# The low part of K on VectorE instead of GpSimd, in an attention and mixture-of-experts block of 32 examples

## What is computed

```python
h = layernorm(x) * (1 + ca) + sa
q, k, v = rotate(rot_w[0], h), rotate(rot_w[1], h), rotate(rot_w[2], h)
attn = softmax((2 + 2 * (q @ k.T)) / scale + bias)
ave = attn @ v
x = x + ga * ave / norm(ave)
h = layernorm(x) * (1 + cb) + sb
x = x + gb * (routed_experts(h, top_k(softmax(h @ gate_w.T))) + shared(gelu(h @ Wsg.T) * (h @ Wsu.T)))
```

## Time and profile before

| what | us |
|---|---|
| median of 3 executions | 2378.26 |
| lowest and highest | 2375.60 and 2378.57 |
| the profiled execution | 2380.66 |
| its span, first to last instruction | 2378.6 |
| TensorE busy in it | 2233.8 |
| VectorE busy | 1660.2 |
| GpSimd busy | 1470.9 |
| ScalarE busy | 1158.4 |

### The profile page before, as it was taken

One profiled execution on the slowest core, in us unless ns is written; L12 is line 12 of the kernel. 1 busy time (PEld: TensorE's weight loads), 2 busy tenths in 40 slices (PEclk: granted clock), 3 DMA queues, 4 the chain that ended last, 5 costly groups with the idle time before them and its releaser, 6 DMA issues.

```text
span 2378.6 us, 40049 instructions
## 1 busy us (share of the span) xinstructions
PE 2233.8 (94%) x13432; PEld 1954.5 (82%) x13432; DVE 1660.2 (70%) x3117; ACT 1158.4 (49%) x2138; POOL 1470.9 (62%) x1156
## 2 busy tenths in 40 slices
PE   5799999999999999999989999999999999999997
PEld 4688888888788878888878888888888888888886
DVE  6788888999999999999765554545555554554543
ACT  4566666667666666566443333333333333333332
POOL 3666666666766766766545666666666666666664
PEclk8899999999999999999999999999999999999999
DMA  3212112122122112112154443444443444443433
GB/s 100 72 57 74 71 64 76 65 70 75 58 74 80 57 68 84 58 69 75 55 124 83 87 86 59 87 90 83 89 87 58 85 89 83 88 88 58 86 62 45
DMA packets 83202, 179.59 MB, mean 76 GB/s; under 512 B 12320, under 2 KB 47296, under 8 KB 83072
## 3 DMA queue, kind: packets, MB, share of 16 engines
q0 software_dynamic: 49152, 67.14, 17.7%
q1 hardware_dynamic: 33600, 109.98, 13.6%
q10 hardware_dynamic: 320, 0.56, 0.1%
HBM read 110.29 MB, written 67.34 MB: 75 GB/s over the span
## 4 chain that ended last, share of the span: by engine, by line
PE 57%; POOL 20%; issue 12%; DVE 7%; ACT 3%; DMA 1%; POOLq 0%; DVEq 0%; ACTq 0%; SPq 0%
PE ps L385 17%; PE ps L386 17%; PE ps L387 17%; DVE stage L1071 3%; POOL x_rows L1397 3%; POOL v_f L1356 3%; POOL weights L1374 3%; POOL v_f L1362 3%; POOL hidden L1341 2%; PE ps L538 2%; PE ps L473 1%; POOL rstd L1350 1%; POOL out_factor L1427 1%; PE ps L426 1%; ACT weights L716 1%
## 5 line engine op out<-in xcount | busy, mean ns | idle before, releaser
L385 PE MATMUL ps<-x_t,weights 128*128 128x512 f32 x1536 | 611.3, 398 | 11.1 <-DVE hidden_f L1305 4.2
L1441 POOL DMA_INDIRECT out<-x_rows,step_token x256 | 418.4, 1634 | 324.0 <-DVE x_rows L1285 265.2
L386 PE MATMUL ps<-x_t,weights 128*128 128x512 f32 x1536 | 600.9, 391 | 0.0
L387 PE MATMUL ps<-x_t,weights 128*128 128x512 f32 x1536 | 599.6, 390 | 0.0
L385 PE MATMUL ps<-weights,hidden 128*128 128x256 f32 x2048 | 585.2, 286 | 4.9 <-DVE hidden L1312 2.3
L386 PE MATMUL ps<-weights,hidden 128*128 128x256 f32 x2048 | 580.6, 284 | 0.0
L387 PE MATMUL ps<-weights,hidden 128*128 128x256 f32 x2048 | 580.5, 283 | 0.0
L1305 DVE TENSOR_TENSOR hidden_f<-gelu,ps 128x512 f32<-128x512 f32 x256 | 175.6, 686 | 385.8 <-ACT gelu L868 385.8
L868 ACT ACTIVATE gelu<-ps 128x512 f32<-128x512 f32 x256 | 152.4, 595 | 551.6 <-PE ps L387 551.6
L385 PEld LDWEIGHTS ps<-weights,hidden 128*128 128x128 f32 x2048 | 393.3, 192 | 15.5 <-issue 2.9
L386 PEld LDWEIGHTS ps<-weights,hidden 128*128 128x128 f32 x2048 | 393.5, 192 | 7.3
(11 more groups left out here) (160 smaller groups left out, 3838.2 us busy)
## 6 DMA issues: line engine op xcount, KB each, us to landing
pairs<-mod_rows SPq DMA_DIRECT2D x36, 512.0 KB, 3.7
x_rows<-in_x SPq DMA_DIRECT2D x32, 512.0 KB, 3.5
h_rows<-stage SPq DMA_DIRECT2D x32, 512.0 KB, 2.6
out<-y_rows SPq DMA_DIRECT2D x32, 512.0 KB, 2.8
value_mods<-value_rows SPq DMA_DIRECT2D x32, 384.0 KB, 3.4
stage<-in_wg SPq DMA_DIRECT2D x16, 512.0 KB, 3.6
stage<-in_wd SPq DMA_DIRECT2D x16, 512.0 KB, 6.2
stage<-in_wu SPq DMA_DIRECT2D x16, 512.0 KB, 4.9
```

What stands on the lines that cost most here:

```text
L385: pe.matmul(o, lhs(HI), rhs(HI), start=start, stop=False)
L386: pe.matmul(o, lhs(HI), rhs(LO), start=False, stop=False)
L387: return pe.matmul(o, lhs(LO), rhs(HI), start=False, stop=stop)
L1441: pool.indirect_dma_start(out=out_rows, out_offset=bass.IndirectOffsetOnAxis(ap=ICUR[g][:, t:t + 1], axis=0), in_=X1[:, g % 2, t * D:(t + ...
```

## The change

`k_split_lo` moves from GpSimd's program to VectorE's. On GpSimd it stood behind the sum into `y_rows` (L1415) and ahead of the factor (L1427); on VectorE it stands behind `hidden(i - 1, 0)` and ahead of the early rounds and `out_norm`. The semaphores and the waits on both sides stay. 31 subtractions of 128x1024 move, those for examples 1 to 31.

```diff
+            def k_split_lo(n):
+                dve.wait_ge(k_hi, n + 1)
+                split_lo(K_FLAT[:, LO, :], K_F[:, :, :].rearrange("p k s -> p (k s)"),
+                         K_FLAT[:, HI, :]).then_inc(k_lo, 1)
...
                 if valid(i - 1):
                     hidden(i - 1, 0)
+                if valid(i + 1) and not at(i, -1):
+                    k_split_lo(i + 1)
                 if at(i, B):
                     first_weights_lo((0, 2), 5)
                 for g, r, before in early:
...
-            def k_split_lo(n):
-                pool.wait_ge(k_hi, n + 1)
-                pool.tensor_tensor(K_FLAT[:, LO, :], K_F[:, :, :].rearrange("p k s -> p (k s)"),
-                                   K_FLAT[:, HI, :].bitcast(F32), ALU.subtract).then_inc(k_lo, 1)
...
-                if valid(i + 1) and not at(i, -1):
-                    k_split_lo(i + 1)
                 if valid(i):
```

More of the change, by code:

```diff
@@ L1231, in iteration @@
                     h1_split_lo(0)
-                    dve.wait_ge(k_hi, 1)
-                    split_lo(K_FLAT[:, LO, :], K_F[:, :, :].rearrange("p k s -> p (k s)"),
-                             K_FLAT[:, HI, :]).then_inc(k_lo, 1)
+                    k_split_lo(0)
                 if at(i, 0):
```

## The result

| what | before | changed |
|---|---|---|
| median, us | 2378.14 | 2383.81 |
| lowest and highest | 2375.60 and 2379.66 | 2381.28 and 2388.09 |
| executions | 8 | 8 |
| the profiled execution | 2380.66 | 2381.28 |
| its span | 2378.6 | 2379.2 |

The ratio of the changed kernel to the one before is 1.0031, with a 95% interval of 1.0021 to 1.0041. It is **slower**, by 5.7 us between the medians (which alone make 1.0024). By this sample the growth is just beyond the 0.2% of the likeliest case, so the second case came true and not the first, which had the higher chance.

A forecast was written before the change was run, and what follows sets the result against it. Regular iterations were taken as bound by ScalarE's squares, iterations 0, 18 and 26 to 30 by VectorE. Terms -1.0 + 4.2 + 1.0 + 0 = +4.2 us on a median of 2378.26 gave 2382.5 us, range 2376 to 2387.

The forecast's parts named there:

- the likeliest case: The terms as summed: 2382.5 us, with 2377.1 to 2383.0 within 0.2% of the time before; chance 54%.
- the second case: The shift passes whole in iterations 18 and 26, 1.06 us each, small start gain: +6.2 us, 2384.5 us, slower; 39%.
- GpSimd's share of the chain is not a gain: Regular iterations: removing 31 subtractions of 2.407 us from GpSimd is worth nothing, since its next operation waits for norm_sq.
- The norm chain waits for the squares: Regular iterations: norm_sq's operation still waits for ScalarE's squares, leaving VectorE 1.0 us of slack; term 0.
- L1041's block: VectorE's 128x4 operation stood blocked behind GpSimd's subtraction, 2.33 us against 0.15.
- Iterations 27 to 30: VectorE is late there and the 1.06 us shift reaches TensorE's wait: 4.2 us slower in all, bounds 1.6 to 4.6.
- The start: Iteration 0, bound by VectorE: unblocked v_cross lets norm_sq's operation start earlier, 1.0 us faster, bounds 0 and twice that.
- Iterations 18 and 26: Early round, no late one: later hidden and score_rows delay TensorE by 0.5 us each, 1.0 us slower; bounds 0.3 and 1.06 each.
- The sum: -1.0 + 4.2 + 1.0 + 0 = +4.2 us, by the ends of the terms -1.2 to +6.7.
- The second rival: Same as the second case: +6.2 us, decided if iterations 18 and 26 cost more than 0.8 us each; 39%.
- The third rival: GpSimd's row is what matters, so 74 us go, to about 2304 us; 2%.
- The fourth, the lock: Regular iterations: L1041 no longer blocked gains 1.0 us in each of 24, 25 us in all, 2353 us; 1%.

The follow-up runs named there:

- not_early: Changed kernel, but the subtraction stays on GpSimd in iterations 18 and 26 to 30 and moves in the other 25; 2377.42 us against 2378.36, ratio 0.9994.
- twice: Changed kernel plus one more equal subtraction on VectorE, into an unread buffer, in the 24 regular iterations; 2385.53 us against 2378.79 before the change, ratio 1.0028.
- thrice: Changed kernel plus two more equal subtractions on VectorE, into unread buffers, in the 24 regular iterations; 2418.20 us against 2378.79 before the change, ratio 1.0160.
- only_early: Changed kernel, but the subtraction is on VectorE only in iterations 18 and 26 to 30; 2385.00 us against 2378.36 before the change, ratio 1.0028.
- again: The changed kernel measured and profiled once more, no edit; 2383.07 us against 2378.36 before the change, ratio 1.0022.
- after_rstd: Changed kernel with the second layer norm's factor moved ahead of v_shift on GpSimd; 2378.90 us against 2377.75 before the change, ratio 1.0004.
- fill: Changed kernel, but the subtraction is on VectorE only in iteration 0; 2377.55 us against 2378.36 before the change, ratio 0.9995.
- behind_norm: Changed kernel with the subtraction behind out_norm instead of ahead of it in every iteration; 2378.63 us against 2378.79 before the change, ratio 1.0000.
- control: Kernel before the change with only GpSimd's iterations unrolled in the code, same order of work; 2376.90 us against 2378.79, ratio 0.9995.
- mix: Changed kernel with the subtraction ahead of out_norm in iteration 0 and behind it elsewhere; 2378.62 us against 2377.75 before the change, ratio 0.9998.
- mix_rstd: Kernel mix with the second layer norm's factor also moved ahead of v_shift on GpSimd; 2373.63 us against 2377.75 before the change, ratio 0.9984.
- before_rstd: Kernel before the change with only the second layer norm's factor moved ahead of v_shift on GpSimd; 2374.35 us against 2377.75, ratio 0.9983.

## Why the prediction was right, and where it wasn't

**GpSimd's share of the chain is not a gain: right.** 31 subtractions left GpSimd and no iteration from 2 to 17 or 19 to 25 moved by more than 0.02 us. `not_early` shows it alone.

**The norm chain waits for the squares: right.** L1049's bracket names them in 25 iterations. The slack of 1.0 us was measured as a wait of 1.04 us; `twice` used it up and `thrice` overran it.

**L1041's block was GpSimd's subtraction: right.** It takes 0.15 us now, 0.16 at most, in all 32. As the prediction said, this alone is worth nothing where the squares are late, and 0.9 us in iteration 0.

**Iterations 27 to 30: right in place, cause and size.** 1.14, 1.12 (28 taken as 29, without the clock), 1.12 and 0.94 us, 4.3 in all where the sum had 4.2. `only_early` gives the same within 0.02 us.

**The start: mis-sized.** The term was -1.0. The first transposes came 0.91 us earlier, but 0.50 were given back in iteration 1, so the term was -0.4. The prediction took the whole gain to come off because TensorE waits 8.1 us there, and expected that wait to shrink to 7.1; it grew to 8.53. What follows it runs at the low level of the clock, and the end of that stretch did not come earlier with its start: the granted clock is 0.50 up to 78.9 us in both traces. Since `only_early` has nearly as much without the move, the 0.50 us is not shown to belong to the change.

**Iterations 18 and 26: mis-sized.** The term was 0.5 us each, 1.0 in all, and measured 1.60 and 0.21. The argument for 0.5 was that TensorE stood ahead of the scores of iteration 18 for 0.34 us of "issue" with no semaphore, so that a later `score_rows` would be absorbed in part. It was not: with `score_rows` 1.2 us later TensorE waits 0.82 us for it by name. In the trace of before the wait was over or nearly so when TensorE came, and a wait that ends in time leaves no bracket. Slack has to be read from the two ends: 708.96 + 1.08 = 710.04 us for `score_rows` and 710.79 for the scores, 0.75 us apart. But in the changed kernel, where TensorE waits for `score_rows` by name, its scores too start 0.66 us behind the end of it (710.15 + 1.07 = 711.22, and 711.88). So of the 0.75 us only 0.09 was slack, and `not_early`, with VectorE 0.35 us late and no bank wait, loses 0.54. Of the 1.60 us the hole in VectorE's row is 0.3 to 0.4: `only_early` and `twice` have none and grow by 1.32 and 1.24. It stands in none of the prediction's steps; the other 1.2 to 1.3 us are still more than twice the term. In iteration 26 the scores come 1.04 us later as well, but the idle time ahead of L1071 takes in 0.8 of it. The prediction priced the two by one wait, that at the scores, and looked at none behind it. This is read from the traces; no run takes that idle time away.

**The clock: missing.** 1.46 us in iteration 28. No term, no rival had it. Every trace with the subtraction on VectorE ahead of the early rounds has such a stretch in iterations 28 to 30 (the changed kernel, `again`, `only_early` and `after_rstd` in 28, `twice` in 30, `thrice` in 29 and 30; `after_rstd` has another in 31), and of the others only `fill` has one between iterations 2 and 31.

**The sum.** -0.4 + 0.1 + 1.6 + 0.2 + 4.3 + 1.5 = 7.3 us against +4.2. The three misses all went the same way: 0.6 at the start, 0.8 in 18 and 26, 1.5 by the clock. The second rival had +6.2 and named iterations 18 and 26 and a small gain at the start as what would decide. Together 18 and 26 cost 1.81 us where it had 2.1, and the start gave little, but not in its way: the shift passed whole in 18 only, and the clock, which it didn't have, did more than either. That the measured median still lies 1.3 us from the forecast is in part luck: stage A of the traces grew by 3.1 us more than the sum, and the medians by 1.5 more.

The third rival, by which the chain was right, is refuted by `not_early`: 25 subtractions left GpSimd and the time stayed. The fourth, the lock, holds in iteration 0 alone, as it was put.

**What stays open.** The hole of 0.48 us in iteration 18: `changed` and `again` have it behind MAX8, `not_early` and `behind_norm` have 0.35 us elsewhere in the same round, `control`, `fill`, `only_early` and `twice` have none. `after_rstd` has it as the changed kernel has, and `mix` and `mix_rstd` have it as `behind_norm` has. So it repeats wherever VectorE's program is the same, and no semaphore accounts for it; that it is how the program lies in memory is a guess which no run tests. And what makes the clock fall: the stretches at the start of an iteration stand behind waits of 1.95 to 2.3 us, and `fill` has one behind 1.77 us, while `behind_norm` and `mix` have waits of 1.78 us, the changed kernel one of 2.00 and `thrice` two of 2.14, without one. A longer wait makes it likelier in these traces, but the six stretches in the middle of iterations of `thrice` follow two waits of 0.76 and some 0.7 us close together. What decides is not settled.

## What to carry to other kernels

An operation is free or costs its full length by its place in the row, not by the engine's load: look for the wait that it can stand in, and then go through the iterations that differ from the rule, since six odd ones here cost more than 25 regular ones could give. Moving work off an engine gains nothing where its consumer waits for a third party, and the bracket that will be left is found by comparing the ends of all that the consumer waits for. A wait that isn't in a trace is not slack: work it out from when the producer ended and from how long the engine takes from a release to its start (0.66 us here, of 0.75 that looked free). Then look at the next wait behind it, which may take the shift in, as in iteration 26, or not, as in 18.

## What the hardware showed that was not expected

**A tiny operation pays the whole price.** On VectorE, 128x4 took 2.33 us in place of 0.15, and in `before_rstd` 128x2 took 2.37 in place of 0.28, each until a GpSimd operation of 2.4 to 2.7 us had ended.

**Two VectorE operations in a row shut GpSimd out once.** The factor was held by the first of two 1.22 us operations and ended while the second ran at its usual length. The Trainium skill (page "SBUF — State Buffer", section "Who interferes with whom") says that a VectorE instruction with two SBUF inputs contends with a GpSimd one that reads SBUF, by an exclusive lock on the shared ports; that the first to issue has them for the whole instruction while the other blocks it says of VectorE's two-port modes. With the first subtraction the trace agrees with such a lock: 1.93 us for the factor against 1.01 alone. Were the lock held for the whole of the factor too, the second VectorE operation, which starts at 596.26, should have stood still until the factor's end at 597.22; it ended at 597.48 after its usual 1.22 us. So here a lock for the whole instruction is not what is measured.

**TensorE's clock falls in the middle of a dense kernel.** Behind a wait of 1.96 us the granted clock of the next 4.4 us was 0.61, and transposes that take 2.8 us took 4.3. In `thrice` nine regular iterations had a lower clock, and that made nearly a third of its loss. In stage B such stretches come and go from trace to trace, with its code unchanged. So a small delay of TensorE may cost more than itself, and two profiles have to be compared by their clock before their spans are.
